# An R-GNN, attention and ternary FFN kernel: products of an item reordered, weight sets moved on VectorE, FFN copies ahead of the gelus

## The reference

```
xn = layernorm(x)
h   = relu(xn @ Wself0 + mean_of_neighbours(xn) @ Wneigh0 + b0)
gnn = h @ Wself1 + mean_of_neighbours(h) @ Wneigh1 + b1
mix = (relu(q) relu(k)^T / (l*64)) v  per head, then @ Wo + bo       # linear attention, 16 heads
x   = x + gnn + mix
f   = quant(gelu(quant(layernorm(x)) @ ternary(w1)^T)) @ ternary(w2)^T   # 1024 -> 4096 -> 1024
out = x + f
```

## Time and profile before

| | |
|---|---|
| time before, median of 3 | 1304.35 us (1303.76 to 1305.66) |
| profiled execution, time / span | 1304.18 / 1302.4 us |
| TensorE busy | 1290.4 us (99%) |
| VectorE / ScalarE / GpSimd busy | 845.7 (65%) / 652.0 (50%) / 93.9 (7%) |
| granted clock of TensorE | 1.000 of full speed |
| matmuls that waited for z0_lo, line 1663, in all | 0.8 us |
| for a first-item copy (787.95) and for T3 (791.98) | 0.24 and 1.26 us |
| DMA share of the 16 engines, 862 to 898 us | 1.0 or more in each 3 us |

### The profile page before, as it was taken

One profiled execution on the slowest core, in us unless ns is written; L12 is line 12 of the kernel. 1 busy time (PEld: TensorE's weight loads), 2 busy tenths in 40 slices (PEclk: granted clock), 3 DMA queues, 4 the chain that ended last, 5 costly groups with the idle time before them and its releaser, 6 DMA issues.

```text
span 1302.4 us, 18781 instructions
## 1 busy us (share of the span) xinstructions
PE 1290.4 (99%) x6370; PEld 613.4 (47%) x6370; DVE 845.7 (65%) x1472; ACT 652.0 (50%) x895; POOL 93.9 (7%) x91
## 2 busy tenths in 40 slices
PE   9999999999999999999999999999999999999999
PEld 5454444555445444444444444444444444444444
DVE  6854542362677778975992663336787977786774
ACT  7766564364312246632442763547863376465460
POOL 0000000000000002100000110133440100000000
DMA  8498987764135466715877999999859939722523
GB/s 355 146 275 268 281 288 199 298 212 167 74 114 193 160 207 217 225 67 185 267 245 243 193 248 214 254 313 314 277 164 372 262 75 280 176 61 83 129 58 104
DMA packets 203093, 269.10 MB, mean 207 GB/s; under 512 B 110464, under 2 KB 144000, under 8 KB 199424
## 3 DMA queue, kind: packets, MB, share of 16 engines
q1 hardware_dynamic: 190432, 255.93, 62.8%
q10 hardware_dynamic: 11136, 6.82, 2.5%
q0 software_dynamic: 1440, 5.24, 2.2%
HBM read 184.33 MB, written 57.67 MB: 186 GB/s over the span
## 4 chain that ended last, share of the span: by engine, by line
PE 93%; DVE 3%; DMA 2%; issue 1%; ACT 1%; POOL 0%; ACTq 0%; SPq 0%; DVEq 0%
PE ps L2252 36%; PE ps L2533 13%; PE ps L2574 12%; PE ps L2684 9%; PE ps L2647 9%; PE ps L2383 8%; PE ps L2452 3%; PE ps L2391 1%; PE ps L2304 1%; DMA w1q_scratch<-STREAM 1%; PE ps L2286 1%; DMA SPLIT<-in_Wself 1%; DMA XIN<-in_x 0%; DVE Zb L1344 0%; PE ps L2729 0%
## 5 line engine op out<-in xcount | busy, mean ns | idle before, releaser
L2252 PE MATMUL ps<-S,XH 128*128 128x512 f16 x1440 | 317.1, 379 | 0.8 <-DVE Zb L1663 0.8
L2252 PEld LDWEIGHTS ps<-S,XH 128*128 128x128 f16 x1440 | 139.8, 98 | 165.7 <-DVE Zb L1663 2.7
L2252 PE MATMUL ps<-S,Zb 128*128 128x512 f16 x480 | 106.4, 379 | 0.0
L2383 PE MATMUL ps<-XH,S 128*128 128x512 f16 (+1 forms) x576 | 102.6, 340 | 0.0
L2252 PE MATMUL ps<-Zb,XH 128*128 128x512 f16 x432 | 94.8, 379 | 0.0
L1003 ACT ACTIVATE AT<-ps 128x320 f16<-128x320 f32 x40 | 17.4, 434 | 140.0 <-PE ps L2252 139.8
L2533 PE MATMUL ps<-XH,AT 128*128 128x512 f16 x400 | 86.8, 379 | 0.0
L2533 PE MATMUL ps<-Zb,AT 128*128 128x512 f16 x400 | 86.5, 379 | 0.0
L1616 DVE TENSOR_SCALAR STREAM<-tables,keys 128x320 f16 x240 | 71.1, 296 | 22.5 <-PE ps L2452 13.3
L2383 PEld LDWEIGHTS ps<-XH,S 128*128 128x128 f16 x576 | 56.0, 98 | 47.1 <-issue 2.3
L2252 PEld LDWEIGHTS ps<-S,Zb 128*128 128x128 f16 x480 | 46.9, 98 | 54.5 <-issue 0.6
(11 more groups left out here) (317 smaller groups left out, 1989.9 us busy)
## 6 DMA issues: line engine op xcount, KB each, us to landing
STREAM<-in_w_all SPq DMA_DIRECT2D x48, 512.0 KB, 5.1
STREAM<-in_w1t SPq DMA_DIRECT2D x42, 512.0 KB, 5.1
STREAM<-in_w2t SPq DMA_DIRECT2D x30, 512.0 KB, 5.1
XIN<-in_x SPq DMA_DIRECT2D x20, 512.0 KB, 5.1
Zb<-in_w1t SPq DMA_DIRECT2D x14, 512.0 KB, 7.2
blocks_scratch<-S SPq DMA_DIRECT2D x4, 1792.0 KB, 8.5
blocks_scratch<-STREAM SPq DMA_DIRECT2D x4, 1792.0 KB, 8.6
S<-blocks_scratch SPq DMA_DIRECT2D x7, 1024.0 KB, 14.4
```

The source lines that it names most:

```text
L2252: last = mm(acc[:, n * BANK:(n + 1) * BANK], left(l, kc), right(kc, r)[:, n * BANK:(n + 1) * BANK], start=(kc == 0 and i == 0), stop=(kc = ...
L2383: last = mm(ps[:, 3 * j * BANK + a:3 * j * BANK + b], Wq_s[:, kc, l, mc], XH[:, r, kc, a:b], start=(kc == 0 and l == 0 and r == 0), stop=( ...
```

## The change

What it does, part by part:

- TensorE's order in the first item (i = 0): P1 of item 1 goes whole between P6 and P7, P2 of item 1 goes between P5 and P3. Before, P1 of item 1 was cut in two halves, behind P7 and behind P5, and P2 of item 1 came after P4 of item 0.
- ScalarE: the first item's copy 0 goes ahead of the last Square; copies 1 and 2 stay behind it.
- VectorE in z0: z0_lo(t) goes ahead of source_sum(4 + t).
- VectorE in the st stage: the third set of an item goes from ahead of c12(i) to behind c11(i + 1), and z1_lo_rest(i) from behind c11(i + 1) to the end of item i.
- FFN, G = 2: ScalarE makes all six copies before any gelu, with y_round(8) and y_std(9) among them and y_round(9) behind four gelus. VectorE's steps wait for the copies at their new counts; hid_ints(1, 2..3) goes into x2_scaled(8), x2_ints(9) into G = 3.
- FFN, G = 4: VectorE's second sums go ahead of sums(1, 0) and sums(1, 1).

```diff
         def st_done(i, product):
 
+            if i == 0:
+                return dict(P1=1, P2=2, P6=3, P7=5, P5=6, P3=8, P4=9)[product]
             if product == "P1":
-                return 7 * i - 1 if i else 1
+                return 7 * i - 1 if i > 1 else 4
+            if i == 1 and product == "P2":
+                return 7
...
+                    if t == NT - 1:
+                        act.wait_ge(S("c_x"), 1)
+                        st_copy(0, 0)
                     A(banks(4), TMP[:, j, :], ACT.Square, accum_out=at("h_sq", t)).then_inc(S("h_sq"), 1)
                 if p == PAIRS - 1:
-                    act.wait_ge(S("c_x"), 1)
-                    for which in range(3):
-                        st_copy(0, which)
+                    st_copy(0, 1)
+                    st_copy(0, 2)
...
+            def f1_act_second():
+
+                G, p, t = 2, 1, 2
+                act.wait_ge(S("dq1"), t + 2)
+                for s in range(2):
+                    f1_copy(G, s, 1 + s, 0, 0, 8 * p - 4)
+                for s in range(2):
+                    f1_copy(G, s, 4 + 2 * s, 1, 0, 8 * p)
+                y_round(8)
+                y_std(9)
+                for s in range(2):
+                    f1_copy(G, s, 8 + 2 * s, 1, 1, 8 * p)
+                for s in range(2):
+                    act.wait_ge(S("f1_ps"), 14 * G + 11 + 2 * s)
+                    gelu(t, 1, s, F1_BANKS[s][0])
+                for s in range(2):
+                    act.wait_ge(S("f1_d"), 6 * G + 1 + s)
+                    alone(act)
+                    gelu(t, 0, s)
+                y_round(9)
+                for s in range(2):
+                    act.wait_ge(S("f1_d"), 6 * G + 3 + s)
+                    alone(act)
+                    gelu(t + 1, 1, s)
+                for s in range(2):
+                    act.wait_ge(S("f1_d"), 6 * G + 5 + s)
+                    alone(act)
+                    gelu(t + 1, 0, s)
...
-            f1_act(1, 0, [lambda: y_round(9)], [lambda: y_round(8), lambda: y_std(9)])
+            f1_act_second()
...
-                if t == 0:
-                    z0_lo(0)
                 if t < NT - 4:
+                    z0_lo(t)
                     source_sum(4 + t)
...
-                if t > 0:
+                if t >= NT - 4:
                     z0_lo(t)
...
                 quads = list(ST_QUADS[i])
                 c11(i)
-                if i > PAIRS:
-                    z1_lo_rest(i - 1)
+                for n in list(ST_QUADS[i - 1])[2:]:
+                    quad(n)
                 ahead = 0 if i == 2 else 1
                 for n in quads[:ahead]:
                     quad(n)
                 if i >= PAIRS:
                     z1_lo_first(i)
                 c22(i)
-                for n in quads[ahead:]:
+                for n in quads[ahead:2]:
                     quad(n)
                 c12(i)
                 c21(i)
+                if i >= PAIRS:
+                    z1_lo_rest(i)
...
-            z1_lo_rest(2 * PAIRS - 1)
+            for n in list(ST_QUADS[2 * PAIRS - 1])[2:]:
+                quad(n)
...
-            x2_scaled(8, lambda: x1_add(9))
+            x2_scaled(8, lambda: (x1_add(9), hid_ints(1, range(2, 4))))
             x1_stats(9)
             x2_ints(8, 0)
-            hid_ints(1, range(2, 4))
-            f1_dve(1, 0, later(x2_scaled, 9), later(lambda: None), later(x2_ints, 9, 1))
-            f1_dve(1, 1, *(later(sums, 0, n) for n in range(2)), *(later(hid_max, 1, 0, 0, h) for h in range(2)))
+            f1_dve(1, 0, later(x2_scaled, 9))
+            f1_dve(1, 1, lambda: (x2_ints(9, 1), sums(0, 0)), later(sums, 0, 1),
+                   *(later(hid_max, 1, 0, 0, h) for h in range(2)))
...
-                f1_dve(p + 1, 0, *(later(sums, p, n) for n in range(3)))
+                if p == 1:
+                    f1_dve(2, 0, later(lambda: None), later(lambda: None), *(later(sums, 1, n) for n in range(2)))
+                    sums(1, 2)
+                else:
+                    f1_dve(p + 1, 0, *(later(sums, p, n) for n in range(3)))
...
+                if i == 0:
+                    st_first(1)
                 st_product(i, "P7", c, stop=False, part=halves[0] if final else range(KC // 2))
-                if i == 0:
-                    st_first(i + 1, halves[0])
                 pe.wait_ge(S("st_act"), 3 * i + 2)
                 st_product(i, "P5", a, False, False)
                 if final:
                     st_product(i, "P7", c, False, False, halves[1])
+                elif i == 0:
+                    st_second(1)
                 else:
-                    st_first(i + 1, halves[1] if i == 0 else range(KC // 2))
+                    st_first(i + 1)
...
-                    wait(pe, "f1_act", 14 * (G - 1) + 10 + 2 * s)
+                    wait(pe, "f1_act", 14 * (G - 1) + (7 + s if G == 3 else 10 + 2 * s))
...
-                    pe.wait_ge(S("f1_act"), 14 * G + 7 + s)
+                    pe.wait_ge(S("f1_act"), 14 * G + (5 if G == 2 else 7) + s)
```

More of the change, by code:

```diff
@@ L2042, in f1_sum @@
                 piece = [hid[:, r, h * 2 * D + j * BANK:h * 2 * D + (j + 1) * BANK] for r, h in ((0, 0), (1, 1), (1, 0))]
-                product, copied = ((3 + 2 * s, 1 + s), (7 + 2 * s, 7 + s), (12 + 2 * s, 3 + 2 * s))[step - 1]
+                product, copied = ((3 + 2 * s, 1 + s), (7 + 2 * s, (5 if G == 2 else 7) + s),
+                                   (12 + 2 * s, 3 + (1 if G == 2 else 2) * s))[step - 1]
                 dve.wait_ge(S("f1_ps"), 14 * G + product)
@@ L2064, in hid_max @@
             def hid_max(p, g, r, h):
-                dve.wait_ge(S("f1_act"), 14 * (2 * p + g) + {(0, 0): 6, (0, 1): 12, (1, 1): 11, (1, 0): 14}[r, h])
+                G = 2 * p + g
+                gelus = {(0, 0): 10, (0, 1): 8, (1, 1): 12, (1, 0): 14} if G == 2 else \
+                    {(0, 0): 6, (0, 1): 12, (1, 1): 11, (1, 0): 14}
+                dve.wait_ge(S("f1_act"), 14 * G + gelus[r, h])
                 wait(dve, "g_max", 2 * p - 1 + r)
@@ L2583, in _, with st_first, st_second @@
             halves = (range(KC // 4), range(KC // 4, KC // 2))
-            def st_first(i, part=range(KC // 2)):
+            def st_first(i):
                 wait(pe, "st_c", 4 * (i - 2) + 3)
-                st_product(i, "P1", st_banks(i)[0], stop=False, part=part)
-            def st_pe(i):
-                a, b, c = st_banks(i)
+                st_product(i, "P1", st_banks(i)[0], stop=False)
+            def st_second(i):
                 wait(pe, "st_c", 4 * (i - 2) + 1)
@@ L2595, in st_pe @@
                     pe.wait_ge(S("h_sq"), NT)
-                st_product(i, "P2", b)
+                st_product(i, "P2", st_banks(i)[1])
+            def st_pe(i):
+                a, b, c = st_banks(i)
+                if i != 1:
+                    st_second(i)
                 pe.wait_ge(S("st_act"), 3 * i + 1)
```

## The result

The changed kernel takes 1329.35 us (median of 6 runs, 1327.30 to 1331.28) beside 1303.57 us for the kernel before on the same chip: ratio 1.0195, 95% interval 1.0181 to 1.0208, or 25.4 us more. The prediction was 1322.0 with a range of 1309 to 1326. The sign and the place were right; the measured time lies 7.4 us above the forecast and 3.4 above the range.

The account below looks back on a forecast made before the run. TensorE, busy nearly all the span, bounds the kernel, with some 8 us about the most to win. Terms -0.6 + 13.5 + 3.0 + 3.5 - 1.6 = +17.8 us on 1304.18 give 1322.0, range 1309 to 1326.

Parts of the forecast that it names:

- the loop: St stage, c11 to c11 through SP's store and next load: 21.9 us against TensorE's 18.13; term +13.5.
- L1749 to the store: St stage, third set's operation (L1717 before) to its store's issue: 5.37 us, 3.5 if VectorE and GpSimd take no turns.
- load issue to both halves landed: St stage, first set's load behind the third's store, with waking ScalarE: 6.1 or 4.9 us, 5.8 taken.
- The turns: St stage, third set: VectorE and GpSimd take turns, 1.9 us of the 5.37; rival without them 1314, chance 0.15.
- The clock: TensorE after its gaps: the prediction had no term for a lower granted clock.
- P4 of item 9, +1.4: End of the st stage: P4(9) waits for c22(9) until 977.9, where it could start at 976.5.
- The x1 stage, +3.0: After the st stage: quad 29 behind z1_lo_rest(9) delays x1's first row block, so edge_sum(2) waits; bounds 0 to +5.
- G = 2 and 3, +3.5: FFN: two gaps go (2.44), but x2_scaled(9) delays P4 and ScalarE's order delays P6 of G = 3; bounds +1, -2.4.
- G = 4, -1.6: FFN: both second sums stand ahead of sums(1,0), so P4 of s = 0 starts when due.
- z0 and the first item: Z0: fourth tile on time, z0_pe(8) earlier, -0.6; first item: TensorE's 1.84 lead is not kept, term zero.
- z0's second count of 0.6: Sum: z0's 0.6 taken off once more although the start of P5 in item 6 already left z0 out.
- queue fuller: Rival for SP's loads: each load 1 us later still, x1 5 late, 1327 or more; chance 0.06.

Follow-up runs that it names:

- pauses made on purpose: Kernel before, with ScalarE repeating the copy that P5 waits for 5, 7, 9 and 13 times more in items 1 to 4: 1327.47 us (one run).
- the kernel with the loads ahead: Changed kernel, with SP from item 6 on issuing the load for the next item's first set ahead of the third set's store: 1315.36 us, ratio 1.0094.
- quad 29 back in its item: Last third set put ahead of c12(9) again, against the changed kernel with next-item loads issued ahead of the third set's store: 1315.44 us, ratio 1.0099.

## Why the prediction had the loop right, and which of its steps failed

**The loop.** One round of the changed kernel, item 7 to item 8, in the prediction's own steps. VectorE's rows (L1743 starts as c11 ends), SP's queue, and ScalarE's start:

```profile
926.04 1.22 DVE L1743 TENSOR_SCALAR SPLIT<-SPLIT 128x2048 f32<-128x2048 f32 x1
...
928.55 1.23 DVE L1749 TENSOR_TENSOR STREAM<-STREAM 128x1024 fp8e4<-128x1024 fp8e4 x1
...
948.96 1.22 DVE L1743 TENSOR_SCALAR SPLIT<-SPLIT 128x2048 f32<-128x2048 f32 x1
```

```profile
933.93 0.52 SPq L510 DMA_DIRECT2D w2q_scratch<-STREAM  x1
934.49 1.78 SPq L500 DMA_DIRECT2D HL<-in_w2t  x2
936.61 0.52 SPq L510 DMA_DIRECT2D w2q_scratch<-STREAM  x1
```

```profile
941.45 2.37 ACT L1041 ACTIVATE HL<-HL,cols 128x1024 f32<-128x1024 f32 x2 [5.46 <-DMA HL<-in_w2t]
```

| step | predicted | round 1 | round 2 | round 3 |
|---|---|---|---|---|
| two operations ahead of L1749 | 2.52 | 2.51 | 2.51 | 2.51 |
| L1749 to the store | 5.37 | 5.38 | 5.38 | 5.38 |
| store to load | 0.57 | 0.57 | 0.56 | 0.56 |
| load to ScalarE | 5.8 | 7.32 | 6.96 | 8.44 |
| ScalarE's start to the end of c11 | 7.6 | 7.52 | 7.51 | 7.51 |
| round | 21.9 | 23.30 | 22.92 | 24.40 |

Four of five steps are within 0.1 us. **The step that failed is "load issue to both halves landed"**, mis-sized by 1.5, 1.2 and 2.6 us, 5.3 in all. Its nearest row, a load directly behind a store, gave 6.1, and the prediction took 5.8: 0.9 of the 5.3. In that row the next store came 2.9 us behind the load, and here it comes 2.1 behind it; moving that store away gave back 2.6, and left 6.15 and 6.26 in two rounds, the 6.1 of the row. What makes the third round's load longer isn't settled. In its stretch the loads land after 7.0 us in the median and the stores after 5.9, against 6.3 and 5.9, and 5.3 and 5.4, in the rounds ahead of it.

**The turns** of VectorE and GpSimd came as priced. GpSimd's first operation on the third set starts 0.16 us after VectorE's L1746 (the L1714 of before) and lasts past its end, and then L1749 (the L1717 of before) takes its turn:

```profile
929.70 1.22 DVE L1746 TENSOR_SCALAR STREAM<-HL 128x2048 fp8e4<-128x2048 f32 x1
930.95 2.00 DVE L1749 TENSOR_TENSOR STREAM<-STREAM 128x1024 fp8e4<-128x1024 fp8e4 x1
```

```profile
929.86 2.01 POOL L775 TENSOR_TENSOR STREAM<-STREAM 128x512 fp8e4<-128x512 fp8e4 x1 [10.45 <-DVE STREAM L1749]
```

GpSimd's operation takes 1.10 alone, so it stood some 0.9 us behind L1746, the operation of which the rows before showed nothing. L1749 takes 2.00 where it takes 1.23 with GpSimd idle, so it stood 0.8 behind GpSimd's. The rule that the prediction cited from the Trainium skill (page "SBUF — State Buffer", section "Who interferes with whom") has this order; the trace agrees.

**The clock** is the second step that failed: the prediction put nothing for it and gave no reason. After the gap before P5 of item 9 it cost 2.2 us. After the gap before item 7's it cost nothing in the end: the loop, not TensorE, set when P5 of item 8 could start, and the gap there was the shorter by it (2.67 after 5.00). In G = 2 and 3 it cost 1.7 us twice: from P4 of s = 0 to the first product of G = 3 there are 4.29 us, 2.59 before, and from P6 of G = 3 to f2 11.19, 9.49 before. Altogether 5.6 of the 27.1 us. The pauses made on purpose show that a pause of TensorE is enough for it.

**P4 of item 9, +1.4** did not show, because the clock hid it. By the prediction's own steps c22(9) ends 9.35 us after c11(9), at 982.7 (it ended at 982.4); P4 was due at 981.2 with P5 at full clock, and at 983.4 with P5 2.2 us slower, where it started. In the kernel with the loads ahead, where the clock didn't fall in item 9, the wait is there, 1.10 us.

**The x1 stage, +3.0** was right in the sum, in part by luck, and wrong in the place. SP's load of XIN and VectorE's start on it:

```profile
997.29 1.72 SPq L632 DMA_DIRECT2D XIN<-u_scratch  x2
```

```profile
1003.00 1.28 DVE L2012 SCALAR_TENSOR_TENSOR TMP<-ps,cols,XIN 128x1024 f32<-128x1024 f32 x1 [8.71 <-DMA XIN<-u_scratch]
```

The load was issued 11.3 us and VectorE had its data 17.0 us after TensorE's end of the stage, not 12.7 and 19.0, so edge_sum(2) waited 0.93. But VectorE works nearly without a pause from there to the FFN (48.3 of 53 us busy from 1003 to 1056), so its delay was still there 57 us later and came out before P6 of G = 0, 1.53 us: 2.7 together. The prediction had closed the account at the first gap. It also put the lateness down to quad 29's place behind z1_lo_rest(9), and that failed: with quad 29 back in its item the load is still issued 11.2 us after TensorE's end of the stage (7.0 before). Both gaps come with the third sets' move; which of item 9's sets holds the load up isn't settled.

**G = 2 and 3, +3.5**: without the clock 3.4. P4 of s = 0 starts 12.74 us after the first product of G = 2, 11.96 before (+0.8, predicted 0.7); P6 of G = 3 is 5.1 later, 1.7 of it clock.

**G = 4, -1.6** came as predicted (-1.5).

**z0 and the first item** came out as forecast in sum, in part by luck. In z0 TensorE gained 0.7 us (589.29 to 675.82, before 588.06 to 675.32): z0's fourth tile starts without a gap, and z0_pe(8) waits 0.28. But this execution entered z0 1.2 us later than that of before; over all kernels here, none of which is changed ahead of z0, the entries lie between 588.1 and 590.7. The lead of TensorE goes at the weight block of item 5, 1.28 us. From there TensorE is due at P5 of item 6 at 904.10, and the copy that P5 waits for ends at 904.06, so two limits meet where the prediction had reckoned with the second alone (904.3).

So the 27.1 - 17.8 = 9.3 us are the loads' 5.3 and the clock's 5.6, less P4's 1.4 and 0.3 in x1 with G = 0, with z0's second count of 0.6 and -0.5 in the small differences of the other steps. Of the rivals, "queue fuller" (1327 or more) had longer loads, which came, and too small a chance; its other half, x1 5 us late, did not come.

## What to carry to other kernels

When a move puts an operation whose result is stored in front of one whose operand is loaded, follow SP's queue once round the loop and compare that period with TensorE's work per item; four terms of such a sum can be read from the trace to 0.1 us, but a DMA's landing has to be bounded by the traffic that the new order puts on both sides of it. When a gap goes with a move, see whether the engine that waited has become later itself. Price a TensorE gap of a few us with what follows it as well as its length. An engine that has no idle time carries a delay on, past the first place where it shows.

## What the runs showed of the hardware

The length of the gap before a product of the st stage and the time of its 12 matmuls (2.76 us at full clock), over these kernels:

| gap, us | 12 matmuls, us |
|---|---|
| 0.90, 1.36, 1.79, 2.11 | 2.76, 2.76, 2.76, 2.75 |
| 2.23 | 4.45 |
| 2.67 | 2.76 |
| 2.99, 3.23, 3.82, 4.08 | 4.45, 4.29, 5.30, 5.30 |
| 4.67, 4.69, 5.00, 5.32 | 5.30, 4.36, 4.71, 4.80 |
| 6.45, 6.70, 7.39, 7.55 | 5.00, 4.56, 4.93, 4.96 |

In these rows gaps up to 2.1 us left the clock at its upper level and those above 3.1 all brought it down. Between them it went both ways. Before P4 of G = 2 in the FFN a gap of 3.00 did nothing, one of 3.03 did nothing in one kernel and cost 1.7 us in another, one of 3.09 cost 1.7 and one of 2.99 cost 1.5. Before P6 of G = 3 three gaps of 2.61 brought the clock down and one did not; that one is the only one without a gap of 3 us 8 to 10 us ahead of it. The cost of one fall, 1.4 to 2.9 us, doesn't follow the gap's length. The Trainium skill (page "TensorE: Matmul & The Clock Gate", section "HAM oscillation — how this bites in real kernels") says that idle gaps of TensorE bring the lower clock back; the rows agree for every gap above 3.1 us, and show it for some shorter ones.

A load took 0.7 to 1.2 us longer from issue to use with a store issued 2.1 us behind it in the same queue than without, in three rounds of one execution of each kernel.
